# Twelve attention heads on one core: two heads share one product with the plain edge counts, and accumulating transfers add up a head's parts

## What is computed

```python
ft = einsum('nhd,od->nho', hv, W)                # 12 heads of 64 columns
a1 = sum(ft * attn_l, -1); a2 = sum(ft * attn_r, -1)
e = leaky_relu(a1[src] + a2[dst], 0.2)
w = exp(e - segment_max(e, dst)[dst])
agg = segment_sum(w / denom[dst] * ft[src], dst) # denom = segment_sum(w, dst)
out = relu(agg + residual)                       # x is added afterwards
```

## Time and profile before

| | us |
|---|---|
| median of 3 runs | 1000.03 (999.43 to 1001.99) |
| the profiled execution | 999.84 |
| its span in the trace | 998.0 |
| the heads' products, first to last | 277.2 (164.6 to 441.8) |
| PE busy, share of the span | 98% |
| DVE busy within the heads | 270.87 of 277.20 |

### The profile page before, as it was taken

One profiled execution on the slowest core, in us unless ns is written; L12 is line 12 of the kernel. 1 busy time (PEld: TensorE's weight loads), 2 busy tenths in 40 slices (PEclk: granted clock), 3 DMA queues, 4 the chain that ended last, 5 costly groups with the idle time before them and its releaser, 6 DMA issues.

```text
span 998.0 us, 15944 instructions
## 1 busy us (share of the span) xinstructions
PE 978.0 (98%) x5726; PEld 792.6 (79%) x5726; DVE 597.3 (60%) x1280; ACT 312.3 (31%) x890; POOL 67.5 (7%) x135
## 2 busy tenths in 40 slices
PE   8999999999999999999899999999999999999998
PEld 6777678999999999986566666666998557988895
DVE  8987899999999999996233238551111111432422
ACT  3444354655565566444101112221111111101101
POOL 2100000000000000123122210000000000000000
PEclk9999999999999999999999999999999999999999
DMA  6000010111111111008582439114001003411002
GB/s 164 2 1 1 1 57 18 36 39 39 43 45 46 48 45 38 14 22 293 167 324 96 152 148 302 56 51 147 1 1 47 1 1 89 113 32 31 16 16 64
DMA packets 40172, 70.00 MB, mean 70 GB/s; under 512 B 21103, under 2 KB 25205, under 8 KB 39602
## 3 DMA queue, kind: packets, MB, share of 16 engines
q1 hardware_dynamic: 37423, 58.81, 18.7%
q0 software_dynamic: 2080, 10.23, 3.0%
q10 hardware_dynamic: 611, 0.20, 0.1%
HBM read 50.10 MB, written 19.12 MB: 69 GB/s over the span
## 4 chain that ended last, share of the span: by engine, by line
PE 89%; DVE 7%; issue 1%; ACT 1%; DMA 1%; POOL 0%; DVEq 0%; SPq 0%; POOLq 0%
PE O L983 19%; PE pw L1161 16%; PE pw L1225 7%; PE pa L1190 7%; PE pc L851 7%; PE O L980 7%; PE ph L1076 5%; PE py L1100 5%; PE pw L1254 4%; PE pa L1237 4%; PE pf L816 2%; DVE ohs_a L1645 2%; PE pt L1149 1%; PE pf L851 1%; DVE ohd L1642 1%
## 5 line engine op out<-in xcount | busy, mean ns | idle before, releaser
L983 PE MATMUL O<-X,masks 125*125 125x260 f32 x1200 | 276.6, 329 | 0.0
L980 PE MATMUL O<-X,CSR 125*125 125x130 f32 x1080 | 244.6, 227 | 0.0
L983 PEld LDWEIGHTS O<-X,masks 125*125 125x125 f32 x1200 | 221.3, 187 | 0.1
L1838 DVE SCALAR_TENSOR_TENSOR masks<-a2b,NA,CSR 125x375 fp32r<-125x375 f32 (+1 forms) x360 | 211.6, 650 | 5.6 <-PE O L983 4.3
L980 PEld LDWEIGHTS O<-X,CSR 125*125 125x125 f32 x1080 | 203.6, 189 | 0.0
L2103 DVE SCALAR_TENSOR_TENSOR UL<-pw,dinv,UH 125x768 fp32r<-125x768 f32 x20 | 20.4, 1018 | 107.7 <-ACT UH L1564 107.7
L1161 PE MATMUL pw<-W 128*125 128x384 f32 x240 | 79.1, 486 | 0.8 <-ACT W L1557 0.8
L851 PE MATMUL pc<-ohs_a,ohd 125*125 125x512 f16 x375 | 77.4, 345 | 0.8 <-DVE ohs_a L1645 0.8
L1161 PE MATMUL pw<-region,xr_or_h 128*125 128x384 f32 x240 | 77.6, 486 | 0.0
L1161 PEld LDWEIGHTS pw<-region,xr_or_h 128*125 128x125 f32 x240 | 45.0, 188 | 32.1
L1645 DVE TENSOR_SCALAR ohs_a<-iota,srcf 125x1250 f16<-125x1250 f16 x128 | 69.6, 544 | 0.0
(11 more groups left out here) (259 smaller groups left out, 1434.4 us busy)
## 6 DMA issues: line engine op xcount, KB each, us to landing
a2b<-a_rows SPq DMA_DIRECT2D x12, 610.4 KB
W<-in_L_ffn_W SPq DMA_DIRECT2D x4, 1152.0 KB, 6.5
WM<-in_L_ffn_W SPq DMA_DIRECT2D x4, 1152.0 KB, 10.2
xr_or_h<-in_x SPq DMA_DIRECT2D x10, 336.0 KB
XH<-in_x SPq DMA_DIRECT2D x12, 280.0 KB
z_rows<-region SPq DMA_DIRECT2D x10, 336.0 KB
region<-y_rows SPq DMA_DIRECT2D x10, 336.0 KB
x_rows<-xr_or_h SPq DMA_DIRECT2D x10, 336.0 KB
```

Source lines behind the costliest of these rows:

```text
L980: nc.tensor.matmul(O[0:P, bank, d - d0, 2 * DP:4 * DP], CSR[:, s, d * P:(d + 1) * P], X[:, buf, s, 4:6, :].rearrange("p k d -> p (k d)"), ...
L983: ins = nc.tensor.matmul(O[0:P, bank, d - d0, 0:4 * DP], kept, X[:, buf, s, 0:4, :].rearrange("p k d -> p (k d)"), start=s == 0, stop=s == ...
L1838: nc.vector.scalar_tensor_tensor(masks[:, s, 0:(d1 - d0) * P], a2b[:, buf, d0 * P:d1 * P], NA1[:, s, bass.ds(h, 1)], CSR[:, s, d0 * P:d1 * ...
```

## The change

1. **Pairs.** Heads 1 and 2, 3 and 4, up to 9 and 10 form pairs; heads 0 and 11 stay alone. In the first head of a pair (kind `PAIR`) the product with the plain counts takes the blocks 4 and 5 of both buffers, so of both heads, 260 columns; its sums of the second head are scaled and kept in `ahead`. In the second head (`PAIRED`) there are masked products alone. Products fall from 2400 to 1900 (1200 masked ones of 260 columns, 500 shared of 260, 200 of 130).
2. **Order of the blocks.** X is negated pair (0, 1), then E1 (2, 3), then E2 (4, 5). PSUM columns follow: ahead, minus, sums.
3. **Adding up.** `evict` writes `sums`, `minus` and in a `PAIR` head `ahead` (one more scaled copy per tile). POOL issues transfers that add: `minus` into `sums`, waited for; in a `PAIRED` head then `ahead` into `sums`, waited for; then the low half into the high half (`s_d2`). DVE's `both` and `whole` go, except for the last head in `finish_tiles`.
4. **Order of the queues.** The steps of `combine` go to the third group, behind masks 3, 8 and 9. `low_parts` becomes two operations: the first for the next head behind mask 8 of group 1, the second behind mask 9, but for a `PAIR` head the second stands behind mask 3 of group 0 of that head itself, and PE does not start a `PAIR` head before it. ScalarE's work is written out for a pair. `XH` has one buffer, loaded after the addition of the head before last has read it.
5. Some semaphores share a number with those of the branch that is not taken.

```diff
-        def products(act, h, buf):
-            for s in range(NT):
-                products_of(h, s)
-            products_high(act, h, buf)
+        def products(act, n, h):
+            if not (isinstance(h, int) and h == 0):
+                act.wait_ge(s_lo[n], h)
+            for s in range(NT):
+                product_of(n, h, s)
+        def product_of(n, h, s):
+            nc.scalar.mul(T12[:, n, s, :], FT[:, s, h, :], (E1, E2)[n][:, s, bass.ds(h, 1)]).then_inc(s_t[n], 1)
+        def products_high(act, n, h, buf):
+            act.wait_ge(s_t[n], (h + 1) * NT)
+            nc.scalar.copy(X[:, buf, :, 2 + 2 * n, :], T12[:, n, :, :]).then_inc(s_hi[n], 1)
         def negated(act, h, buf):
+            act.wait_ge(s_lo[1], h + 1)
+            nc.scalar.mul(X[:, buf, :, 0:2, :], X[:, buf, :, 4:6, :].bitcast(F32), -1.0).then_inc(s_xn, 1)
+        def low_part(dve, n, h, buf):
+            dve.wait_ge(s_hi[n], h + 1)
+            nc.vector.tensor_tensor(X[:, buf, :, 3 + 2 * n, :], T12[:, n, :, :],
+                                    X[:, buf, :, 2 + 2 * n, :].bitcast(F32), ALU.subtract).then_inc(s_lo[n], 1)
...
-        ev = sb(quick, "ev", [P, NT, 2, 2 * DP])
-        both = sb(quick, "both", [P, NT, 2 * DP])
-        whole = sb(quick, "whole", [P, NT, DP])
+        sums = sb(quick, "sums", [P, 2, 2, NT, DP])
+        minus = sb(quick, "minus", [P, 2, NT, DP])
+        ahead_raw = sb(quick, "ahead", [P, 2 * NT * DP])
...

                     for h in range(2, H):
                         row(h, h % 2)
-                        x_columns(h)
+                        sp.wait_ge(s_xa, h)
+                        x_columns(h - 1, XH, s_xh)
+                    sp.wait_ge(s_da, 16 * JOBS * (H // 2 - 1))
+                    x_columns(H - 1, XH_last, s_xi)
...
+                def quickly():
+                    def add(h, g, shared):
+                        d = slice(*GROUPS[g])
+                        n = JOBS * h + g + 1
+                        pool.wait_ge(s_ev, n + 2)
+                        nc.gpsimd.dma_start(sums[:, h % 2, :, d, :], minus[:, :, d, :],
+                                            accum_op=ALU.add).then_inc(s_d1, 16)
+                        pool.wait_ge(s_d1, 16 * n)
+                        if shared:
+                            m = JOBS * (h // 2 - 1) + g + 1
+                            nc.gpsimd.dma_start(sums[:, h % 2, :, d, :], ahead[:, :, d, :],
+                                                accum_op=ALU.add).then_inc(s_da, 16)
+                            pool.wait_ge(s_da, 16 * m)
+                            pool.sem_inc(s_af, 1)
+                        nc.gpsimd.dma_start(sums[:, h % 2, 0, d, :], sums[:, h % 2, 1, d, :],
+                                            accum_op=ALU.add).then_inc(s_d2, 16)
+                    pool.sem_inc(s_af, JOBS)
+                    for h in range(H - 1):
+                        for g in range(JOBS):
+                            add(h, g, h >= 2 and h % 2 == 0)
+                    pool.wait_ge(s_d2, 16 * JOBS * (H - 1))
...
+                        def counted(bank, d, d0, s):
+                            c = CSR[:, s, d * P:(d + 1) * P]
+                            if kind == PAIR:
+                                nc.tensor.matmul(O[0:P, bank, d - d0, 0:4 * DP], c,
+                                                 X[:, 0:2, s, 4:6, :].rearrange("p b k d -> p b (k d)"),
+                                                 start=False, stop=False, skip_group_check=True)
+                            elif kind == ALONE:
+                                nc.tensor.matmul(O[0:P, bank, d - d0, 2 * DP:4 * DP], c,
+                                                 X[:, buf, s, 4:6, :].rearrange("p k d -> p (k d)"),
+                                                 start=False, stop=False, skip_group_check=True)
+                        pe.wait_ge(s_lo[0], h + 1)
                         pe.wait_ge(s_xn, h + 1)
+                        if kind == PAIR:
+                            pe.wait_ge(s_lo[1], h + 2)
...
+                    def evict(h, buf, g, kind, pairs=0):
                         act.wait_ge(s_mf, (JOBS * h + g + 1) * NT + NT)
-                        if g == 0:
-                            act.wait_ge(s_evf, h + 1)
-                        nc.scalar.copy(ev[:, d0:d1, 0, :], O[0:P, bank, 0:d1 - d0, 0:2 * DP])
+                        if not (isinstance(h, int) and h == 0):
+                            act.wait_ge(s_d1, 16 * JOBS * h + 16 * (g + 1 - JOBS))
+                            act.wait_ge(s_xa, h)
+                        nc.scalar.copy(sums[:, buf, :, d0:d1, :] ..., O[0:P, bank, 0:d1 - d0, 4 * DP:6 * DP] ...)
                         for d in range(d0, d1):
+                            ins = nc.scalar.mul(minus[:, :, d, :], ..., G2[:, d, bass.ds(h, 1)])
+                        if kind == PAIR:
+                            act.wait_ge(s_af, JOBS * pairs + g + 1)
+                            for d in range(d0, d1):
+                                ins = nc.scalar.mul(ahead[:, :, d, :], ..., G2[:, d, bass.ds(h + 1, 1)])
                         ins.then_inc(s_ev, 1)
...
+                    def pair(q, follows, last=False):
+                        h = 2 * q + 1
+                        evict(h - 1, 0, 2, follows)
+                        products(act, 0, h + 1)
+                        products_high(act, 0, h + 1, 0)
+                        negated(act, h + 1, 0)
+                        evict(h, 1, 0, PAIR, q)
+                        products(act, 0, h + 2)
+                        scale_rows(h - 1, 0)
+                        evict(h, 1, 1, PAIR, q)
+                        evict(h, 1, 2, PAIR, q)
+                        products(act, 1, h + 2)
+                        products_high(act, 1, h + 2, 1)
+                        products_high(act, 0, h + 2, 1)
+                        evict(h + 1, 0, 0, PAIRED)
+                        negated(act, h + 2, 1)
+                        if not last:
+                            products(act, 1, h + 3)
+                            products_high(act, 1, h + 3, 0)
+                        scale_rows(h, 1)
+                        evict(h + 1, 0, 1, PAIRED)
...
+                    def combine(h, buf):
+                        dve.wait_ge(s_d2, 16 * JOBS * h + 16 * JOBS)
+                        k(nc.vector.tensor_scalar(den[:, :], sums[:, buf, 0, :, DH], TINY, None, ALU.max))
                         nc.vector.reciprocal(rec[:, :], den[:, :]).then_inc(s_rec, 1)
                         yield
                         dve.wait_ge(s_nrm, h + 1)
...
+                    def head(h, buf, kind, first=False, final=False):
                         for s in range(NT):
                             mask(h, buf, 0, s)
+                            if kind == PAIR and s == 3:
+                                low_part(dve, 1, h + 1, 0)
...
                             mask(h, buf, 1, s)
+                            if not final and s == 8:
+                                low_part(dve, 0, h + 1, 1 - buf)
+                            if kind != PAIR and not final and s == 9:
+                                low_part(dve, 1, h + 1, 1 - buf)
...
                             mask(h, buf, 2, s)
+                            if s in (3, 8, 9):
                                 next(steps, None)
```

More of the change, by code:

```diff
@@ new lines, in program @@
+        s_t, s_hi, s_lo = ([sem(f"{w}_{n}") for n in ("first", "second")]
+                           for w in ("products", "products_high", "products_low"))
+        def products(act, n, h):
+            if not (isinstance(h, int) and h == 0):
+                act.wait_ge(s_lo[n], h)
+            for s in range(NT):
+                product_of(n, h, s)
+        def product_of(n, h, s):
+            nc.scalar.mul(T12[:, n, s, :], FT[:, s, h, :], (E1, E2)[n][:, s, bass.ds(h, 1)]).then_inc(s_t[n], 1)
@@ L1414, in _ @@
                     if 0 <= n - 156 < NT:
-                        products_of(0, n - 156)
+                        for u in range(2):
+                            product_of(u, 0, n - 156)
                     if n == 170:
-                        products_high(act, 0, 0)
+                        for u in range(2):
+                            products_high(act, u, 0, 0)
                     if n == 195:
@@ L1468, in evict, with scale_rows @@
                         ins.then_inc(s_ev, 1)
-                    def scale_rows(h):
+                    def scale_rows(h, buf):
                         act.wait_ge(s_rec, h + 1)
                         for t in range(NT):
-                            ins = nc.scalar.mul(whole[:, t, 0:DH], whole[:, t, 0:DH], rec[:, t:t + 1])
+                            w = sums[:, buf, 0, t, 0:DH]
+                            ins = nc.scalar.mul(w, w, rec[:, t:t + 1])
                         ins.then_inc(s_nrm, 1)
-                    def head(h, buf, first=False, last=False):
-                        if not first:
```

(32 more changed lines are left out.)

159 lines of the change are left out of this document (68 added, 91 removed).

## The result

The changed kernel takes 1218.37 us in the median of four runs (1217.50 to 1219.29), the kernel before 999.76 on the same chip: ratio 1.2181, 95% interval 1.2160 to 1.2202. The profiled execution has a span of 1216.5 us, 218.5 more than before.

The account below looks back on a forecast made before the run. PE and DVE bound the heads within 2.3%. Heads: 21.4 + 4 x 46.0 + 43.8 + 0.8 + 23.1 = 273.1 us against 277.2; with 1 us behind them, 997, plus 9 for the clock: 1006 us, range 980 to 1036.

Parts of the forecast that it names:

- Bound and products: Heads: PE and DVE bounds within 2.3%; 260-column products at 0.125 us, each shared one saving 0.087 us of PE time.
- Order: Queues within a pair: waits between engines lose the gain, so a pair takes 46.0 +- 0.7 us against 46.2.
- The wait of 2.1 us: Second head of a pair: DVE waits 2.1 us for ScalarE's scaled rows and ends at 45.7 us.
- The start: Before the first pair: ScalarE's late rounding leaves PE idle 1.7 us and puts DVE's pair at 21.4 us.
- case A: Heads: same layout, transfers on time and a clock that holds, 997 us (993 to 1001); chance 0.21.
- Clock: Pair ends: PE idles 6.8 of 7.2 us, its clock falls, and the next head loses 2.2 us, 9 in all.
- case B: The forecast: pairs win nothing and the clock falls between them, 1006 us (1001 to 1014); chance 0.29.
- Transfers: POOL's accumulating transfers: hidden behind the heads if each lands within 3.4 us, with under a microsecond to spare.
- L = 3.0: Landing time in us of one accumulating transfer from its issue, taken from line L748's transfers; bounds 2.5 and 6.
- case C: Transfers set the pace if landing exceeds 3.4 us: 1012 us at 4, 1037 at 5, 1062 at 6; chance 0.25.
- The chain: Five transfer waits from group 1's copy to DVE's reciprocal: up to 5 us per pair per microsecond of landing over 3.4.
- Behind the heads: After the last mask: later `combine`, POOL's constants and single-buffered `XH` loads cost 1 us together.

Follow-up runs that it names:

- the run with fillers: The changed kernel with transfers left out and only their semaphores raised, plus unread 512-column products on PE in each pair's second head: 1005.14 us.
- without transfers: The changed kernel with the accumulating transfers left out, POOL only raising their semaphores, so the output lacks the scaled counts: 1018.44 us, ratio 1.015.
- the kernel with the transfers alone: The changed kernel with its two-row transfers but no group shared and none from `ahead`; ScalarE's scaling and second low part also reordered: 1151.83 us.

## Why the prediction was wrong

**Bound and products: right.** With everything on time the spacing of 260 columns is 0.1225 us (in the changed kernel, from 196.81 to 197.79 eight products apart), against 0.125:

```profile
196.81 0.29 PE L1028 MATMUL O<-X,masks 125*125 125x260 f32 x1
...
197.79 0.28 PE L1028 MATMUL O<-X,masks 125*125 125x260 f32 x1
```

**Order: right for the pair.** 46.0 us a pair was forecast and 46.1 measured, once transfers and clock were taken out. The wait of 2.1 us is there with 2.05. The start was 2.4 us longer than laid out: in the run with fillers the second pair begins 69.8 us behind the first product (234.4 and 164.6 us), where 21.4 + 46.0 was forecast. PE idles for 1.9 us there, as forecast (1.7), but its clock then falls too (0.57 from 191 to 195 us without transfers), which the layout left out. With the 5 us by which the fillers hold up the last head this is nearly all of the way from case A's 997 to the 1005 us of that run.

**Clock: the mechanism right, the sum too small.** The clock did fall at each pair's end, for 10.2 us a time, and costs 1.7 us a pair (47.8 against 46.1) where I took 2.2. Left out was the last head: in the traced run the clock stays at half for 30.7 us there, and PE takes 37.2 us for the head instead of 23.2. These 14 us and the 2 at the start, less 2 by which four pairs were shorter than the forecast 48.2, lead from 1006 to the 1020 us of that run; so case B by itself was worth about 1018 in the median, not 1006, above its range (1001 to 1014).

**Transfers: the step that failed.** It is "I take L = 3.0, the faster row, since neither side is HBM; bounds 2.5 and 6". Measured: medians of 8.0 to 10.5. Three things were in it. The row I took had 128 partitions of one row; these have 125 of two, and the 5 engines that case C mentioned are about what they got. "The additions read their destination too" had no price; adding is a factor of 1.6. The price of packets (80 ns at 1.6 KB) was carried to shorter packets by length, but a packet of 1040 bytes takes about 105 ns here and one of 780 bytes 86 (six under way, 58 starting in a microsecond), so 250 of them took over 4 us in place of my 2 to 4. The upper bound had been made from the price of the data alone, and more came on top. In the transfer issued at 237.78 us the data packets run from 240.8 to 247.1 us: 3 us of issue and start before them, then 6.3 us, the first part of it shared with the 550 small packets.

**The chain: the wrong length.** My slope of 5 us for each microsecond of L failed as well: I counted five waits between the copy of group 1 and the reciprocal. Beyond an L of about 4.5 what counts is all of GpSimd's queue, nine transfers and six issues, since 9 x 4.5 + 6 x 0.9 is 46 us. With L = 9.2, which is itself taken from the measured pair, it gives 88 us a pair; five pairs are 209 us over my layout's 46.0, and 997 + 209 = 1206 us against the 1218.4 measured. That the total comes close is partly luck. By the masks the first pair loses only 16 us (62.5 against 46.9), the other four 169, and the last head, which waits for transfers too, 32 (53.6 against 21.5). The form of the sum could have been had before: each row of it is one issue of GpSimd's queue and one landing.

**The chances.** C had 0.25 and a range cut at L = 5. A transfer of a kind that no row showed, waited for nine times a pair on one queue, deserved the larger share and an open upper end: over the five pairs each microsecond of L was worth 25 us by my own count and 45 by the queue's.

**Behind the heads: about right.** From last mask to the end 564.8 us against 562.8, 2 us where I took 1.

## What to carry to other kernels

Before you move additions to accumulating transfers, count the transfers that one queue must wait for in a round and multiply by a landing time measured on that very shape; lay each transfer out as one contiguous row in each partition. When an optimisation frees an engine, ask whether the next one can follow in that stretch: here sharing one group of three took from PE just what VectorE could keep up with, and the kernel was faster than with all of them shared (the order of two steps differed too). And look at the granted clock behind each new gap of a few microseconds on PE; some products into unused PSUM were worth 13 us in one kernel and 3 in another.

## What the runs showed of the hardware

- A transfer within SBUF over 125 partitions issued by GpSimd had 5 to 6 packets under way with two rows in a partition and some 16 with one: 5.2 against 2.7 us as a plain copy, 8.4 against 4.3 with addition, for the same 190.4 KB. GpSimd's issue itself took 2.0 to 2.4 us with two rows and 0.85 with one; without the addition 1.2 and 0.54.
- With the addition every row of 780 to 2080 bytes was a packet of its own; as a copy most of the data went in packets of up to 4680 bytes.
- PE stayed at half of its clock while busy without a gap for 214 us in the kernel with the transfers alone, and for 30.7 us in and before the last head without transfers, of which it was busy for 30.2. In the changed kernel's pairs and elsewhere it rose again. What lets it rise stays open; that steady work alone brings it back was not so here.
- A wait of 1.96 us on PE behind a stretch of steady work was followed by 10.2 us at half clock. With nine products in the gap, and nothing else changed, the clock held (1.00 from 424 to 456 us).
